# A graph network on one core: more gathered tiles taken from one-hot matrices in layers 2 and 3, whose loads another engine begins

## What is computed

```python
def _genconv(x, src, dst, ea, W1, b1, lg, lb, W2, b2, t):
    m = relu(x[src] + ea) + EPS
    logits = m * t
    mx = segment_max(logits, dst)
    e = exp(logits - mx[dst])
    alpha = e / segment_sum(e, dst)[dst]
    agg = segment_sum(m * alpha, dst)
    h = relu(_ln((agg + x) @ W1 + b1, lg, lb))
    return h @ W2 + b2

h = relu(_layernorm(x))
z = h @ encW + encb ; ea = edge_attr_64 @ eencW + eencb
z = _genconv(z, ..., layer 0)
for i in 1, 2, 3:
    z = z + _genconv(relu(_ln(z, normG[i], normB[i])), ..., layer i)
x = x + relu(_ln(z, normG[0], normB[0])) @ linW + linb
h = relu(_layernorm(x))
return x + segment_sum(h[dst] * edge_weight, src)
```

## Time and profile before

| | us |
|---|---|
| median of 3 runs | 11808.61 (11800.38 to 11816.48) |
| the profiled execution, its own time | 11828.1 |
| its span, first to last instruction | 11826.3 |
| granted TensorE clock, mean over the span | 0.694 |
| full windows of layer 0 | about 170 to 2500 |
| of layers 1, 2, 3 | from 2723, 5109 and 7485 on, with four small windows and a node stage behind |
| weighted sum, after layer 3 | from 9795 on |

### The profile page before, as it was taken

One profiled execution on the slowest core, in us unless ns is written; L12 is line 12 of the kernel. 1 busy time (PEld: TensorE's weight loads), 2 busy tenths in 40 slices (PEclk: granted clock), 3 DMA queues, 4 the chain that ended last, 5 costly groups with the idle time before them and its releaser, 6 DMA issues. The chain is left out here.

```text
span 11826.3 us, 107787 instructions
## 1 busy us (share of the span) xinstructions
PE 5802.2 (49%) x31762; PEld 4077.1 (34%) x31762; DVE 6551.7 (55%) x8055; ACT 3327.1 (28%) x4948; POOL 6522.0 (55%) x6157
## 2 busy tenths in 40 slices
PE   2333333343444444444444444444444447888887
PEld 2222222232333333333333333333333334444443
DVE  5666666664444444544444445444444457998897
ACT  1333333342333333333333333333223232111110
POOL 5455455535444444454544444544444446888887
PEclk6666666666666666666666666666666668999998
DMA  5344344333333333333333333333333334555555
GB/s 155 125 137 138 123 140 132 130 109 103 118 117 117 117 117 117 102 97 116 119 118 118 117 118 106 95 117 118 117 117 117 117 112 94 99 97 99 96 94 86
DMA packets 840467, 1354.58 MB, mean 115 GB/s; under 512 B 499934, under 2 KB 556476, under 8 KB 838730
## 3 DMA queue, kind: packets, MB, share of 16 engines
q1 hardware_dynamic: 523832, 1135.94, 27.5%
q0 software_dynamic: 312640, 214.30, 12.9%
q10 hardware_dynamic: 3916, 3.40, 0.1%
HBM read 806.66 MB, written 546.46 MB: 114 GB/s over the span
## 5 line engine op out<-in xcount | busy, mean ns | idle before, releaser
L826 POOL DMA_INDIRECT xg<-h_tab,idx x4656 | 4461.7, 958 | 4370.0 <-DVE idx L1159 2909.3
L917 PE MATMUL turn<-hb,hot 125*128 125x192 bf16 x12480 | 1872.5, 295 | 3018.0 <-issue 2977.7
L917 PEld LDWEIGHTS turn<-hb,hot 125*128 125x128 fp8e4 x12480 | 1310.6, 114 | 3571.7 <-issue 3536.0
L1159 DVE COPY idx<-idx_full 128x24 int32 x208 | 36.6, 176 | 3526.7 <-ACT zl L1035 3526.7
L933 PE MATMUL turn<-ident,sums 128*128 128x128 f32 x5184 | 1073.7, 375 | 1533.8 <-ACT st_all L1050 1140.4
L1524 POOL DMA_INDIRECT acc<-vm,tgt x1026 | 1602.9, 1562 | 341.2 <-issue 288.1
L933 PEld LDWEIGHTS turn<-ident,sums 128*128 128x128 f32 x5184 | 878.0, 222 | 1676.3 <-ACT st_all L1050 1243.6
L1066 ACT ACTIVATE hx<-turn 128x384 bf16<-128x384 f32 x156 | 76.4, 490 | 3600.9 <-PE turn L917 3553.1
L1050 ACT ACTIVATE st_all<-turn 128x512 f32<-128x512 f32 (+1 forms) x1344 | 752.3, 577 | 698.7 <-PE turn L933 321.0
L1166 DVE TENSOR_TENSOR_SCAN rx<-rp,carry,zl 128x1536 f32<-128x1536 bf16 (+1 forms) x224 | 739.9, 3303 | 360.1 <-ACT zl L1035 343.1
L1597 PE MATMUL zl<-spreadz,lo_hot 128*128 128x512 f32 x1620 | 765.5, 609 | 95.2 <-DVE spreadz L1773 95.2
(11 more groups left out here) (277 smaller groups left out, 7413.2 us busy)
## 6 DMA issues: line engine op xcount, KB each, us to landing
sums<-st_all SPq DMA_DIRECT2D x208, 1536.0 KB
hot<-hot_tab SPq DMA_DIRECT2D x312, 625.0 KB
ea<-feat SPq DMA_DIRECT2D x158, 768.0 KB
srcB<-src_flat SPq DMA_DIRECT2D x108, 768.0 KB
rp<-run_pen SPq DMA_DIRECT2D x210, 384.2 KB
xg<-h_tab,idx POOLq DMA_INDIRECT x4656
hot_tab<-hot SPq DMA_DIRECT2D x104, 625.0 KB
run_head<-zeros SPq DMA_DIRECT2D x216, 192.0 KB
```

What stands on the lines that cost most here:

```text
L826: g_.indirect_dma_start(xg[b][:, k, h, :], None, h_tab[:, :], bass.IndirectOffsetOnAxis(ap=idx[b][:, h, k:k + 1] if small is None else idx ...
L917: ins = pe.matmul(picked[:, :, n % 2, :], hot[n][0:PN, t_, :], hb[0:PN, t_, :, :], start=t_ == 0, stop=t_ == NT - 1, skip_group_check=True)
```

## The change

Layer 2 picks a third tile a window and layer 3 a third and a fourth (`HOT`). The third one-hot matrix of each window is made in layer 1 and the fourth in layer 2 (`MADE_IN`), stored and loaded as the others. All loads but that of a layer's first window are now started from ScalarE's queue, right behind `picked` of the window before; the last pair of windows of its loop is written out, since the last window loads nothing more. The rooms `hot[2]`, `hot[3]` and their columns were there before. In the last layer the node rows aren't stored to `h_tab`; SyncE waits for the last of them instead.

```diff
@@ -70,8 +70,8 @@
 XT = 5
 ROWS = EPAD // W
 ROWS_REAL = E // W
-HOT = [0, 2, 2, 2]
-MADE_IN = [0, 0]
+HOT = [0, 2, 3, 4]
+MADE_IN = [0, 0, 1, 2]
 NHOT = len(MADE_IN)
 ROUNDS = [-(-n // 2) for n in HOT]
 PN = N // NT
@@ -720,13 +720,11 @@
 
                     hot_rows = hot_src.rearrange("r (h w) p -> r h w p", h=2)
 
-                    def load_hot(l, w):
+                    def load_hot(l):
                         for n in range(HOT[l]):
-                            if isinstance(w, int) and w == 0 and n == 0:
+                            if n == 0:
                                 sp.wait_ge(hot_out, out_count(l, 0))
-                            if not (isinstance(w, int) and w == 0):
-                                sp.wait_ge(hot_ps, ps_count(l, w - 1, n))
-                            sp.dma_start(hot_words[n][0:PN, :], hot_tab[n][w]).then_inc(hot_in, 16)
+                            sp.dma_start(hot_words[n][0:PN, :], hot_tab[n][0]).then_inc(hot_in, 16)
 
                     def keep_hot(l, w, b, more):
                         for j, n in enumerate(made(l)):
@@ -755,14 +753,12 @@
                         for n in made(l):
                             for b in range(2):
                                 load_columns(n, b, b)
-                        for w in range(2):
-                            load_hot(l, w)
+                        load_hot(l)
                         with sp.Fori(0, FULL_PAIRS - 1) as i:
                             for b in range(2):
                                 load(l * LW + 2 * i + 2 + b, 2 * i + 2 + b, b, first)
                                 if first:
                                     keep_features(2 * i + b, b)
-                                load_hot(l, 2 * i + 2 + b)
                                 store(l * LW + 2 * i + b, 2 * i + b, b)
                                 clear(l * NW + 2 * i + b)
                                 keep_hot(l, 2 * i + b, b, True)
@@ -795,13 +791,14 @@
                         for b in range(2):
                             sp.wait_ge(feat_out[b], 16 * PAIRS + FT0)
                             load((l + 1) * LW + b, b, b, False)
-                        for k in range(NCH):
+                        for k in range(NCH if l + 1 < L else 0):
                             sp.wait_ge(h_ok, NCH * l + k + 1)
                             store_nodes(k)
 
                     for l in range(L):
                         layer(l, l == 0)
-                    sp.wait_ge(tab_out, 16 * NCH * L + 16)
+                    sp.wait_ge(tab_out, 16 * NCH * (L - 1) + 16)
+                    sp.wait_ge(h_ok, NCH * L)
                     sp.wait_ge(out_lists, 16 * 6)
                     sp.wait_ge(out_tabs, 16 * (2 + ACCS))
                     sp.wait_ge(heads_zero, 16 * L * NW)
@@ -1064,6 +1061,9 @@
                             part = ps[6 + (b + r) % 2][:, 0:6 * D].rearrange("e (s h d) -> e s h d", s=3, h=2)
                             taken = slice(0, n % 2 + 1)
                             a.activation(hx[b][:, r, :, taken, :], part[:, :, taken, :], ACT.Copy).then_inc(hx_sb, 1)
+                        if not (isinstance(w, int) and w == FULLW - 1):
+                            for n in range(HOT[l]):
+                                a.dma_start(hot_words[n][0:PN, :], hot_tab[n][w + 1]).then_inc(hot_in, 16)
 
                     def layer(l):
                         g0 = l * LW
@@ -1074,7 +1074,7 @@
                         exponentials(g0)
                         preload(g0 + 1, 0, l, 1)
                         picked(1, l, 1)
-                        with a.Fori(0, FULL_PAIRS - 1) as i:
+                        def pair(i):
                             for b in range(2):
                                 w = 2 * i + b
                                 logits(g0 + w + 1, i + b, l, 1 - b)
@@ -1082,6 +1082,10 @@
                                 exponentials(g0 + w + 1)
                                 preload(g0 + w + 2, i + 1, l, b)
                                 picked(w + 2, l, b)
+
+                        with a.Fori(0, FULL_PAIRS - 2) as i:
+                            pair(i)
+                        pair(FULL_PAIRS - 2)
                         logits(g0 + FULLW - 1, FULL_PAIRS - 1, l, 1)
                         empty(g0 + FULLW - 2, FULL_PAIRS - 1, l, 0)
                         exponentials(g0 + FULLW - 1)
```

## The result

The changed kernel takes 12483.94 us (median of 4 runs, 12459.78 to 12497.27), the kernel before on the same chip 11807.31 us (4 runs). The ratio is 1.057, with a 95% interval from 1.0551 to 1.059: 676.6 us more. The prediction was 12265 us with a range from 11880 to 12820, slower with a chance of 0.88. The direction came out, and so did the main mechanism; the size is 219 us short, and one term carries most of that.

The account below looks back on a forecast made before the run. Bound: TensorE's picking, stalled until some 4 us after the last gather, then a chain. +0.7, +2.8 and +5.4 us a window in layers 1 to 3 over 51 windows, +458 with starts and end, gave 12265 us; range 11880 to 12820.

Parts of the forecast that it names:

- The stall is tied to the gathers' end: Picking in layers 2 and 3: fewer gathers end TensorE's stall earlier, -1.3 and -2.5 us a window.
- All added pairs land behind the stall, and the clock rises while they pass: TensorE's picking: added pairs are uncovered, +4.2 us a window in layer 2 and +7.6 in layer 3.
- Late is not lost: Picking after later loads: what starts late would have stalled anyway; -1 us a window in layers 2 and 3, +0.3 in layer 1.
- My upper bounds, +2 and +4 us: Late loads in layers 2 and 3: most lost a window if the loads end after the gathers.
- ScalarE's issues: Load issues ahead of ScalarE's mask, on the chain: +0.4, +0.9 and +1.3 us a window in layers 1, 2, 3.
- Making and storing at nothing: VectorE's making and the stores in layers 1 and 2: hidden by idleness, 0, up to +1 us a window.
- My sum of the high bounds: Whole kernel with every bound high: 51 x (2.2 + 8.9 + 17.0) + 30 = +1460 us.
- Starts of layers: First pickings of a layer wait for more loads, while gathers end sooner: +5 us in all, between -8 and +30.
- The last store of node rows: End of the last layer: dropping SyncE's store gives -1.5 us, between 0 and -3.
- Rival A: Layers 1 to 3: clock stays at 0.50 and loads end after the gathers; +1390 us, 13200; chance 0.21.
- Rival B: Layers 2 and 3: late picking escapes the stall, kernel faster; -660 us, 11150; chance 0.08.
- Rivals C and D: Picking: C, added pairs go at the stall's speed, near 21000, chance 0.04; D, no difference, 11830, chance 0.05.

Follow-up runs that it names:

- experiment 1: Kernel before with the third and fourth tile and their matrices made, but SyncE issuing all loads early as before: 12236.23 us, ratio 1.0361.
- experiment 3: Kernel before with all added tiles and SyncE's loads, begun only when the picking with the last matrix is done: 12366.72 us, ratio 1.0458.
- experiment 8: Changed kernel with matrix tables of 128 rows in place of 125: 12578.69 us, ratio 1.0615 with the stall; 8690.03 us, ratio 0.9903 without.
- experiment 2: Changed kernel with two tiles a layer as before, loads still issued by ScalarE, last node rows not stored: 11966.62 us, ratio 1.0124.
- the kernel of 20 wide pairs: Kernel before with 20 pairs of 384 columns a picking instead of 40 of 192: 11371.51 us, ratio 0.9595 with the stall; 8776.24 us without.
- experiment 7: Changed kernel loading only the first two matrices, added pairs and making kept: 9213.72 us, ratio 1.0496, on the chip without the stall.
- experiment 4: Kernel before with one picked tile instead of two in layers 1 to 3, second matrix not made in layer 0: 11709.23 us, ratio 0.9895.

## Why the prediction was right in kind and short in size

- **The stall is tied to the gathers' end: right.** It ends 31.3, 29.9 and 28.4 us behind the first gather. -1.4 and -2.9 us, predicted -1.3 and -2.5.
- **All added pairs land behind the stall, and the clock rises while they pass: right.** With SyncE's early loads (experiment 1) 62 and 101 pairs stand there, 44 and 83 more than before, and the rest grows by 3.7 and 7.8 us. Predicted were 40 and 80 pairs and 4.2 and 7.6 us. The split came out the other way round: I had 0.105 us a pair for the first 40 and 0.085 for the next, measured were 0.085 for the first 44 and 0.104 for the next 39, so that each sum came out closer than its parts deserve. The rows of experiment 1 show the clock go from 0.50 to 1.00 behind the stall. In the changed kernel a pair behind the stall takes 8.1 / 70 = 0.12 and 10.8 / 115 = 0.09 us.
- **"Late is not lost", -1 us in layers 2 and 3: this step failed, in layer 2 in its sign.** The rest grew by 0.85, 5.05 and 7.65 us, where my terms together (pairs plus late loads) gave 0.3, 3.2 and 6.6. That is 0.5, 1.9 and 1.0 us a window, about 175 us over 51 windows, and most of the 219. I took the first picking of a layer, which got 80 pairs through the earlier trace rows, for a sign that a late picking passes more. In the windows it passes slightly less ahead of the stall (44 and 43 pairs for 48), and it forgoes those that crawl through (6 and 2 for 14). By the difference between experiments 1 and 3 lateness costs 0.5, 1.2 and 0.7 us a window, 121 us; experiment 8, which removes it from the changed kernel itself, gives 0.4, 0.9 and 0.5 us of rest. In layer 3 the sign is open: against experiment 1 the rest of the changed kernel is 0.1 us shorter, since the 14 pairs more behind the stall cost what the earlier rise of the clock gives back. There the credit of 1 us was not lost but never came. My upper bounds, +2 and +4 us, held it.
- **ScalarE's issues, +0.4, +0.9 and +1.3 us: right.** The chain grew by 0.6, 1.1 and 1.4 us, about 0.35 us an issue (1.06 for three, 1.45 for four), not 0.46, and the copy hides hardly any of it. The difference between the changed kernel and experiment 3 is 117 us, where my terms make 51 x 2.6 = 133; the chain alone makes 157, and the clock behind the stall in layer 3, better here than in experiment 3, gives part of it back.
- **Making and storing at nothing: nearly right.** Layer 1 of experiment 1 is 0.37 us a window above before, inside the bound of +1. (My sum of the high bounds has this +1 for layer 1 and forgot it for layer 2; that is 51 us on +1460 and leaves the range as it is.)
- **Starts of layers, +5: somewhat low.** From a layer's last full window to the next one's first it was +6.8, +1.8 and +3.6 us, 12 in all, inside the bound of +30. The first is the one I have no full account of. On ScalarE's timeline the first copy of picked rows in layer 1 comes after all gathers of the first two windows:

```profile
2724.72 0.49 ACT L1063 ACTIVATE hx<-turn 128x384 bf16<-128x384 f32 x1 [49.70 <-remote]
```

  In the trace of before it came at 2688.73, 26 us behind the first gather of the layer and in the midst of them. It is late in experiment 1 too (the passage is +6.8 us there), and not in experiments 2 and 8, so it is not ScalarE's issues; which of the signals of TensorE get through at the start of a layer and which don't stays open.
- **The last store of node rows, -1.5: can't be told.** What stands behind layer 3 is 1.3 us shorter, but in the kernels that keep the store, experiments 1 and 3, it is 2214.7 and 2210.0 us long, against 2213.0 before and 2211.6 after.
- **Rival A** (clock and lateness both bad, 13200) had the second of its causes in part. **Rival B**, that a late picking escapes the stall, did not come about, not even 20 us behind the first gather in layer 3: 43 pairs pass there as elsewhere, and 115 start only when the stall is over. **Rivals C and D** didn't come about.

## What to carry to other kernels

Before adding work to an engine that stalls, count what passes ahead of the stall, in instructions, and place the addition against that number: here 80 instructions a window passed free, each pair beyond some 46 cost about 0.1 us, and a version with one tile less in layers 1 to 3 is 2.3% faster than the kernel before, where one and two more in layers 2 and 3 made it 5.7% slower. Starting a transfer later is not free because its reader would have idled anyway; ask what that reader still gets done while it idles. Where a stall shows on some chips only, the sign of such a change can too: try it on more than one.

## What the runs showed of the hardware

**The stall showed on some chips and not on another.** There the same kernel before took 8777.33 us (13 runs, 8770.83 to 8780.5), where it took 11807 to 11851 on the others, and TensorE picks while gathers are made, without a gap. From the changed kernel with tables of 128 rows on that chip, layer 3, TensorE:

```profile
6003.17 14.83 PE L914 MATMUL turn<-hb,hot 125*128 125x192 bf16 x160 [1.76 <-DMA hot<-hot_tab]
```

and GpSimd at the same time:

```profile
6003.49 0.95 POOL L823 DMA_INDIRECT xg<-h_tab,idx  x1 [0.30 <-issue]
6004.75 0.95 POOL L823 DMA_INDIRECT xg<-h_tab,idx  x1 [0.30 <-issue]
```

A gather costs the same 1.26 us there. With two tiles (the kernel of 20 wide pairs) a window is 27.70 us, which is 22 x 1.26, and with one tile 28.97, which is 23 x 1.26: without the stall GpSimd is the bound, and a picked tile is worth its whole gather. With the loads fast, three and four tiles gave 26.56 and 27.30 us a window, and that kernel was 1.0% faster than before; the fourth tile is no gain there, its window is 2.1 us above 20 x 1.26. With slow and late loads, though, TensorE waits for them in layers 1 and 2 (31.43 and 31.89 us a window). The kernel with two loads (experiment 7), layer 1, TensorE:

```profile
2703.07 8.70 PE L914 MATMUL turn<-hb,hot 125*128 125x192 bf16 x80 [11.17 <-DMA hot<-hot_tab]
...
2735.50 9.52 PE L914 MATMUL turn<-hb,hot 125*128 125x192 bf16 x80 [12.34 <-DMA hot<-hot_tab]
```

and the issues of the loads between the two, on ScalarE's queue:

```profile
2711.95 0.71 ACTq L1066 DMA_DIRECT2D hot<-hot_tab  x2
```

From there to the picking it is 22.8 us, where two such loads take 10 by themselves. In layer 3 it is 12.4 us, and a window takes 28.69. So it isn't lateness alone: in layers 1 and 2 a matrix is also made and stored in each window, and which transfer beside the loads stretches them was not tried. Where the stall is, lateness costs some 121 us of 677; where it is not, the kernel with two late loads over few DMA engines is 5.0% slower than before, that with all loads over 16 engines 1.0% faster. What differs between the chips no run shows. The chips of the experiments were four different ones, each used in one stretch of time, so it isn't shown either that the stall stays with a chip.

**What the stall is made of.** In the full windows some 86 to 97 instructions of TensorE (weight loads and matmuls) pass after the picking begins, whether it begins 2.9 or 20 us behind the first gather; 80 pass whole at 192 and at 384 columns; the stall ends 4.0 to 4.9 us after the start of the last gather; and signals from TensorE to ScalarE are held back over the same time. At the start of a layer the number is another one: 80 pairs of the first picking and 21 of the second pass before. The first picking of layer 3 in the changed kernel:

```profile
7763.60 6.55 PE L914 MATMUL turn<-hb,hot 125*128 125x192 bf16 x54 [26.53 <-DMA hot<-hot_tab]
```

and with tables of 128 rows, where the stall is (second run of experiment 8):

```profile
7849.87 11.34 PE L914 MATMUL turn<-hb,hot 125*128 125x192 bf16 x104 [14.73 <-DVE hb L1370]
```

What fits the windows is thus no fixed store, and why the starts differ stays open. All this looks like something that hands TensorE its instructions and carries its signals, and that the gathers hold up. That is a guess, not shown: no row names it.

**Layer 0 has two paces,** 44.5 to 45.1 us a window in most kernels and 47.7 to 47.9 in experiments 4 and 8, which changed only the making of a matrix or the width of its store there. It moved the time by 150 us, more than the whole lateness of the loads. The stall is in it: TensorE's `back` (line 933) from 600 to 2400 us, in the kernel before:

```profile
L933 PE MATMUL turn<-ident,sums 128*128 128x128 f32 x972 | 206.7, 380 | 648.9 <-ACT st_all L1050 397.3 <-issue 251.5
```

and in experiment 4:

```profile
L933 PE MATMUL turn<-ident,sums 128*128 128x128 f32 x897 | 198.2, 383 | 851.1 <-issue 737.3 <-ACT st_all L1050 113.8
```

Ahead of `back` "issue" is 737 us in experiment 4 and 541 in experiment 8, against 223 to 331 in the kernels with the fast pace. Without the stall layer 0 takes 31.5 to 31.6 us a window in all four kernels, that of experiment 8 too. What makes the stall fall on `back` in the one and not in the other stays open.
